# Two-layer GNN on one core: message rows and their places in a ring of eight slots, every scatter plain

## The reference, cut to what matters

```
weight = relu(edge_attr @ W1 + b1) @ W2 + b2      # edge_attr: (206250, 64), weight: (206250, 128)
h      = x @ Wl + bl                              # (6250, 128)
msg    = h[dst] * weight
out    = segment_sum(msg, src, 6250);  x = x + out
```

## Time and profile before

| | us |
|---|---|
| median of 3 runs | 3927.46 (3926.26 to 3931.88) |
| span of the profiled execution | 3952.0 |
| POOL busy | 2311.6 (58%), 1789 instructions |
| PE busy | 3250.2 (82%) |
| DVE busy | 2751.6 (70%) |
| ACT busy | 2038.0 (52%) |
| scatters, line 581 | 1664, the first at 1133.1, the last at 3801.1 |

### The profile page before, as it was taken

One profiled execution on the slowest core, in us unless ns is written; L12 is line 12 of the kernel. 1 busy time (PEld: TensorE's weight loads), 2 busy tenths in 40 slices (PEclk: granted clock), 3 DMA queues, 4 the chain that ended last, 5 costly groups with the idle time before them and its releaser, 6 DMA issues.

```text
span 3952.0 us, 95934 instructions
## 1 busy us (share of the span) xinstructions
PE 3250.2 (82%) x26010; PEld 2424.8 (61%) x26011; DVE 2751.6 (70%) x7605; ACT 2038.0 (52%) x4686; POOL 2311.6 (58%) x1789
## 2 busy tenths in 40 slices
PE   1899999999777778888888888888778787888867
PEld 0566666666555556665666666666566665666656
DVE  8888888888854456666666666666666666666746
ACT  3688788877532224444444444444444443444456
POOL 5200000000247778888888788888888888888830
PEclk9999999999867778998988888899899998899989
DMA  3398988200024457776667667677666676667757
GB/s 103 111 313 309 313 312 312 91 5 2 12 50 84 82 96 149 148 140 123 147 136 147 139 129 144 142 142 148 123 147 140 140 148 120 142 143 145 153 129 204
DMA packets 571932, 569.04 MB, mean 144 GB/s; under 512 B 69768, under 2 KB 555670, under 8 KB 571621
## 3 DMA queue, kind: packets, MB, share of 16 engines
q1 hardware_dynamic: 424950, 446.22, 40.5%
q0 software_dynamic: 146672, 119.07, 20.4%
HBM read 280.17 MB, written 284.85 MB: 143 GB/s over the span
## 4 chain that ended last, share of the span: by engine, by line
PE 50%; issue 16%; DVE 11%; ACT 5%; POOL 5%; another core or an unknown queue 5%; DMA 4%; DVEq 2%; ACTq 0%; POOLq 0%; SPq 0%
PE PS L1085 12%; PE PS L1246 10%; PE PS L1213 7%; PE PS L1225 5%; POOL messages L581 5%; PE PS L1076 4%; PE PS L1202 4%; DMA messages<-big,idxr 4%; ACT big L1425 2%; DVE aux L737 2%; DVE X L986 2%; PE PS L1210 2%; PE PS L1194 2%; ACT H L1429 1%
## 5 line engine op out<-in xcount | busy, mean ns | idle before, releaser
L581 POOL DMA_INDIRECT messages<-big,idxr x1664 | 2145.7, 1290 | 566.8 <-issue 480.1
L1246 PE MATMUL PS<-big,H 128*128 128x128 f32 x4800 | 657.4, 294 | 224.9 <-ACT H L1429 123.7
L1246 PEld LDWEIGHTS PS<-big,H 128*128 128x128 f32 x4800 | 614.0, 207 | 276.6 <-issue 237.9
L1413 ACT ACTIVATE big<-PS 128x512 f32<-128x512 f32 x416 | 248.4, 597 | 1002.4 <-PE PS L1225 615.8
L1085 PE MATMUL PS<-par,aux 128*128 128x386 bf16 x3626 | 682.4, 327 | 0.0
L959 DVE TENSOR_TENSOR big<-PS,big 128x512 f32<-128x512 f32 x416 | 287.3, 691 | 465.5 <-remote 213.0
L1330 ACT ACTIVATE aux<-PS 128x784 bf16<-128x784 f32 x592 | 480.4, 823 | 205.9 <-PE PS L1076 201.2
L1213 PE MATMUL PS<-W2s,big 128*128 128x128 f32 x3328 | 555.6, 317 | 0.0
L1213 PEld LDWEIGHTS PS<-W2s,big 128*128 128x128 f32 x3328 | 466.9, 217 | 109.3 <-issue 109.3
L986 DVE TENSOR_TENSOR X<-X,PS 128x128 f32 x1200 | 345.2, 288 | 247.6 <-PE PS L1246 88.8
L1402 ACT ACTIVATE big<-PS,b1c 128x512 f32<-128x512 f32 x416 | 283.3, 681 | 432.9 <-PE PS L1202 245.3
(11 more groups left out here) (221 smaller groups left out, 3769.9 us busy)
## 6 DMA issues: line engine op xcount, KB each, us to landing
messages<-zeros SPq DMA_DIRECT2D x843, 193.5 KB
big<-messages SPq DMA_DIRECT2D x300, 516.0 KB
aux<-slot_rows SPq DMA_DIRECT2D x416, 128.0 KB
big<-in_edge_attr_dram SPq DMA_DIRECT2D x402, 128.0 KB
messages<-big,idxr POOLq DMA_INDIRECT x1664
X<-in_x_dram SPq DMA_DIRECT2D x6, 448.0 KB, 11.4
out_dram<-X SPq DMA_DIRECT2D x6, 448.0 KB
edge_places<-big SPq DMA_DIRECT2D x1, 2496.0 KB, 13.2
```

The costliest lines, as they stand in the source:

```text
L581: pool.indirect_dma_start(strm_d, bass.IndirectOffsetOnAxis(ap=idxr[:, n % U, j:j + 1], axis=0), outr[:, n % U, j, :], None, compute_op=AL ...
L1246: last = nc.tensor.matmul(to[:, r * C:(r + 1) * C], finhot[:, n % 2, r * 2 + q, :], fin[:, k, r, q * ROW:q * ROW + C], start=(q == 0), sto ...
```

## The change

The rings of `outr` and `idxr` get UO = 8 slots, each with its semaphore, and `outr` moves from the tile `big` to a free piece of `H`. `ADDING` is empty, so all 1664 scatters write plainly. POOL's steps are 8 written out and one loop of 17 rounds of 24. On the other engines `steps` writes out 20 steps instead of 4 at the start of the first part, and its loop makes two rounds of 16 instead of three: the wait on a landed scatter then has a value above zero wherever it stands in a loop. The wait values follow from the eight semaphores. Everything else stays.

```diff
+    UO = 2 * U
+    ADDING = ()
-        idxr = sb("idxr", [P, U, J], i32)
+        idxr = sb("idxr", [P, UO, J], i32)
-        outr = part(big, used, U * J * ROW).rearrange("p (u j c) -> p u j c", u=U, j=J)
+        free_n = H[:, :, :].rearrange("p b c -> p (b c)")
+        outr = free_n[:, 2 * FO * P:2 * FO * P + UO * J * ROW].rearrange("p (u j c) -> p u j c", u=UO, j=J)
-        S_sc = [sem(f"scattered_{k}") for k in range(U)]
+        S_sc = [sem(f"scattered_{k}") for k in range(UO)]
...
         def steps(eng, step, turn=None, rings=RINGS):
-            for s in range(U):
+            for s in range(U + U * rings):
                 step(s, s, None)
             for p, rounds in enumerate(LOOPS):
-                at = U if p == 0 else TURN[p - 1] - 1
+                at = U + U * rings if p == 0 else TURN[p - 1] - 1
+                if p == 0:
+                    rounds = rounds - 1
...
             def part_landed(p):
-                for k in range(U):
-                    sp.wait_ge(S_sc[k], 64 * len(range(k, TURN[p], U)))
+                for k in range(UO):
+                    sp.wait_ge(S_sc[k], 64 * len(range(k, TURN[p], UO)))
...
                 for j in range(J):
-                    pool.indirect_dma_start(strm_d, bass.IndirectOffsetOnAxis(ap=idxr[:, n % U, j:j + 1], axis=0),
-                                            outr[:, n % U, j, :], None, compute_op=ALU.add if j in adding else ALU.bypass).then_inc(S_sc[n % U], 16)
+                    pool.indirect_dma_start(strm_d, bass.IndirectOffsetOnAxis(ap=idxr[:, n % UO, j:j + 1], axis=0),
+                                            outr[:, n % UO, j, :], None, compute_op=ALU.add if j in adding else ALU.bypass).then_inc(S_sc[n % UO], 16)
-            fewer = ((1,), (0, 3))
-            for g in range(U):
-                scatter(g, g, fewer[g % 2])
...
+            for g in range(UO):
+                scatter(g, g, ADDING)
...
+            with pool.Fori(0, (G - UO) // (3 * UO)):
+                for k in range(3 * UO):
+                    scatter(None, UO + k, ADDING)
...
             def row_places(g, n):
-                k, s = n % U, n % 2
+                k, s = n % UO, n % 2
...
-                wait(dve, S_sc[k], (g - k) * 16)
+                wait(dve, S_sc[k], (g - k) * (64 // UO))
                 nc.vector.tensor_copy(idxr[:, k, :], place_f).then_inc(S["rank_chain"], 1)
```

More of the change, by code:

```diff
@@ L32, in gnn_program @@
     GT = T0 // J
-    GL = (GT - 1 - U) // (3 * U)
     XS = T0 - (SB - 1) * P
-    assert GT * J == T0 and G % U == 0 and 0 < XS < P and XS + NB - 1 <= P
+    ADDING = ()
+    assert GT * J == T0 and G % U == 0 and (G - UO) % (3 * UO) == 0 and 0 < XS < P and XS + NB - 1 <= P
     TB = -(-T0 // P)
@@ L215, in gnn_program @@
         fin = part(big, used, 4 * FO * ROW).rearrange("p (s r f) -> p s r f", s=4, r=FO // 2)
-        finhot = H[:, :, :].rearrange("p b c -> p (b c)")[:, 0:2 * FO * P].rearrange("p (s t v) -> p s t v", s=2, t=FO)
+        free_n = H[:, :, :].rearrange("p b c -> p (b c)")
+        finhot = free_n[:, 0:2 * FO * P].rearrange("p (s t v) -> p s t v", s=2, t=FO)
+        outr = free_n[:, 2 * FO * P:2 * FO * P + UO * J * ROW].rearrange("p (u j c) -> p u j c", u=UO, j=J)
         par = sb("par", [P, NB * HW], bf16)
@@ L446, in _ @@
             steps(sp, edge_loads)
-            for k in range(U):
-                sp.wait_ge(S_sc[k], 16 * G)
+            for k in range(UO):
+                sp.wait_ge(S_sc[k], 64 * (G // UO))
             octs(sp, stream_loads)
@@ L566, in _, with scatter @@
             filled = pool.alloc_register("filled")
-            def scatter(g, n, adding=(1, 3)):
+            def scatter(g, n, adding):
                 if not isinstance(g, int):
@@ L580, in scatter @@
                 for j in range(J):
-                    pool.indirect_dma_start(strm_d, bass.IndirectOffsetOnAxis(ap=idxr[:, n % U, j:j + 1], axis=0),
-                                            outr[:, n % U, j, :], None, compute_op=ALU.add if j in adding else ALU.bypass).then_inc(S_sc[n % U], 16)
-            fewer = ((1,), (0, 3))
-            for g in range(U):
-                scatter(g, g, fewer[g % 2])
[L587 to L597, removed]
+                    pool.indirect_dma_start(strm_d, bass.IndirectOffsetOnAxis(ap=idxr[:, n % UO, j:j + 1], axis=0),
+                                            outr[:, n % UO, j, :], None, compute_op=ALU.add if j in adding else ALU.bypass).then_inc(S_sc[n % UO], 16)
+            for g in range(UO):
+                scatter(g, g, ADDING)
+            pool.reg_mov(placed, 5 * UO + 5)
+            pool.reg_mov(lrows, UO + 1)
+            pool.reg_mov(filled, UO + 1)
+            with pool.Fori(0, (G - UO) // (3 * UO)):
+                for k in range(3 * UO):
+                    scatter(None, UO + k, ADDING)
         def dve_link(eng, count):
@@ L958, in messages @@
                 dve.wait_ge(S["hgc_done"], g + 1)
-                nc.vector.tensor_tensor(outr[:, k, :, 0:C], pW[:, k % 2, :].rearrange("p (j c) -> p j c", j=J),
+                nc.vector.tensor_tensor(outr[:, n % UO, :, 0:C], pW[:, k % 2, :].rearrange("p (j c) -> p j c", j=J),
                                         hgs[:, k % 2, :].rearrange("p (j c) -> p j c", j=J), ALU.mult).then_inc(S["msg_done"], 1)
@@ L1406, in local_rows @@
                 act.wait_ge(S["rank_chain"], g * 5 + 5)
-                nc.scalar.activation(outr[:, k, :, C], blcol[:, 1, ds(g * J, J)], ACT.Copy, scale=-1.0).then_inc(S["lrow_ready"], 1)
+                nc.scalar.activation(outr[:, n % UO, :, C], blcol[:, 1, ds(g * J, J)], ACT.Copy, scale=-1.0).then_inc(S["lrow_ready"], 1)
             def rows_copy(g, n):
```

## The result

The changed kernel takes 4419.8 us (median of 4 runs, 4415.3 to 4423.9) where the kernel before takes 3928.2 us on the same chip: a ratio of 1.124 (95% interval 1.123 to 1.126), 12.4% slower. The forecast was 3832 us and the range ended at 3915 us, so the prediction was wrong in sign and size.

What follows compares the result with a forecast made beforehand. POOL's scatters looked like the bound, with the DVE, PE and ACT round next. Gains of 76 (ring wait), 15 (end) and 4 (turns) sum to 95 us: profiled 3952.0 becomes 3857, or 3832 us as median; range 3700 to 3915.

Steps and rivals of the forecast that it cites:

- What bounds the kernel: Layer 1: POOL's scatters look like the bound, 6.43 us a step, with the DVE, PE and ACT round nearly as slow.
- All scatters plain, POOL's cost: POOL in layer 1: 806 scatters fall from 1.56 to 0.97 us, saving 476 us of its time; 5.08 us a step.
- The round behind it: Later steps of layer 1: the DVE, PE and ACT round sets the pace next, near 6.22 us a step.
- Ring wait, half of 151.6 us: DVE's line 953 waiting for landed scatters: eight slots remove it, gaining 76 us (bounds 0 and 151.6).
- The end and the turns: After the last message, POOL's shorter lag saves 15 us; at turns between parts, SP's shorter wait saves 4 of 33.4 us.
- First part: First 52 steps: no gain, as messages already set 6.33 us a step; at most 65 us if wrong.
- DMA: Software queue and DMA engines in layer 1: plain scatters should need less of them; costed at nothing.
- Written-out steps, H, semaphores: Longer straight code, message rows in H, four more semaphores: 0, or 3 us better if a left-out return saves a stall.
- The free run: Rival, layer 1: without ring waits PE's clock rises, 5.5 us a step, 3572 us, half way about 3740; 13 in 100.
- The slower rival: Line 953's waits cover PE lateness that then shows at lines 959 and 986: 6.55 us a step, 3956 us; 8 in 100.

Runs made afterwards that it cites:

- half the rows: The changed kernel with the scatters for j = 2 and 3 left out: 3486.1 us, ratio 0.887 to the kernel before.
- the rests in the middle of a step: Changed kernel, POOL waiting for two memsets behind scatter j = 1 (387 columns, then 16, 128, 230 or 387): 4023.1, 4011.6, 4001.7, 4023.8 us.
- the one at its end: Changed kernel, POOL waiting for one memset of 387 columns behind the last scatter (j = 3) of each step: 4192.6 us, ratio 1.062.

## Why the prediction was wrong

*What bounds the kernel.* "It looks like the bound" was right: POOL is within 57 to 80 us of its floor, and removing the slot wait alone gives 1.000. But I then left this reading for the round of DVE, PE and ACT, on the strength of a sentence that is false, that this round "is nearly as slow as POOL". Free of long rows of scatters it makes a step in 5.53 us. The equal paces in the earlier trace rows were POOL's own pace, or nearly: 50 steps of 6.26 us are 313 of the 320 us.

*All scatters plain, POOL's cost.* Right: 0.97 us, 5.08 us a step.

*The round behind it: the step that failed.* "Everything else that a faster POOL may give must come through them or from the end" treated POOL's choice of scatter as a matter of POOL's time alone, and the round as untouched by it. The sum had no term for it; it put the round at 6.22 us a step. The runs showed a coupling that runs the other way: behind back-to-back plain scatters PE's signals come late (by 1.7 and 5.1 us in the table above), and a step takes 7.68 us. The trace of the kernel before had it in view. Its waits from 1300 to 3700 us hold these lines:

```profile
ACT big L1413 <- remote: 298.3, 98, 5.2
...
DVE big L959 <- remote: 163.0, 85, 5.9
```

One of them is ACT's 5.25 us at 2143.55 us, ended 0.04 us after an adding scatter. The prediction looked at named releasers only and uses none of these.

*Ring wait, half of 151.6 us.* Measured 0 (ratio 1.000, 0.999 to 1.001, with eight slots and adds). The lower bound that I had named was the truth; that the window without the wait was no faster said so.

*The end and the turns.* The end came as forecast: the last scatter ends 5.6 us behind the last message (4261.73 us). But it is worth nothing beside the rest. The first drain load starts 1.5 us after the last scatter's end,

```profile
4266.32 0.96 POOL L585 DMA_INDIRECT messages<-H,idxr  x1 [0.30 <-issue]
4268.73 2.33 SPq L414 DMA_DIRECT2D big<-messages  x4
```

and of the 15 us nothing shows in the run with the ring alone, since there POOL stays behind. The turns fell from 33.4 to 9.4 us without effect on a time that others set.

*First part.* "I take 0, cover: the message round" was wrong by 0.45 us in 52 steps, 23 us slower. POOL's wait for messages there rose from 18.6 to 72.8 us.

*DMA.* "I cost it at nothing" was right for the transfers: packets fell by 62% and the share of the DMA engines from 0.68 to 0.42.

*Written-out steps, H, semaphores.* Nothing, as said; the run with the ring of eight contains all of them. The Trainium skill (Runtime: NRT & Kernel Launch, Instruction fetch mechanics) has a taken branch out of the fetched pages wait for a fetch. No run here shows what the one return that is left out saves: the 3.4 us that a return cost in the earlier trace rows lie within that run's interval of 0.1%.

*The rivals.* The free run put the unhindered round at 5.5 us a step, and half the rows gave 5.53 us; but what hindered it was not the ring's wait. It also tied the clock to PE's waiting: the granted clock is 0.90 in the kernel before, 0.82 in the changed one, where the round waits for late signals, and 0.97 with half the rows. The slower rival had the right sign and the right line (957 waiting for its inputs), but it looked for hidden lateness of PE and priced it at 44 us; the lateness was made by the change itself and cost 492.

*What is shown and what is not.* Shown: the plain scatters alone cause it (ring of four, too); idle time of POOL removes most of it without adds; half the scatters, which means shorter rows and an idle POOL at once, remove it; PE's signals appear in bursts behind such rows, and those of DVE and ACT do not. Argued only: that the products had really run when the profile says so and just their signals were late. The ends of PE's products in the profile are modelled, so they do not prove it. For it speaks that PE's later products are recorded meanwhile and that the signals of several products appear 0.04 to 0.1 us apart (five of them between 2523.30 and 2523.55 us), among them that of the weights, whose product alone takes 1.16 us. Open is by what path POOL's scatters hold up PE and neither DVE nor ACT. It is not the scatter's packets at the DMA engines as far as the times go: behind the rows of four the first signal keeps its 1.0 us after POOL's end while the last packet ends 0.9 to 4 us after it. And why the rests in the middle of a step do more than the one at its end is open.

## What to carry to other kernels

When one engine is the bound because it issues many indirect transfers, making each cheaper also makes its rows denser; look first at whether other engines' waits with an unknown releaser end where its rows, or its slower instructions, end. If they do, the slow instructions may be openings, and the change should be tried at several doses and not all or none. And a wait of an engine that does not set the pace can be worth nothing: 151.6 us of waiting went here and the time stayed the same.

## What the runs showed of the hardware

- A plain indirect scatter of 128 message rows costs POOL 0.97 us and shows 16 packets of 4128 bytes in the trace; an adding one costs 1.56 us and shows 128 packets of 516 bytes.
- Between plain scatters at 1.27 us PE's signals are late by 1.7 us in the median 2 to 4.8 us into a row and by 5.1 us further on; POOL idle: 0.02 us. Those of DVE and ACT come within 0.02 us in either case.
- PE's signals come through about at the end of an adding scatter; with two apart in four the time is 57 to 80 us over POOL's floor, and one (ratio 1.116) is nearly as bad as none (1.124).
- A memset that POOL waits for costs it a gap of 1.14 us with one column and 1.46 us with 387, behind a scatter that ends a step; behind the second scatter 387 columns give 1.23 us and a second such memset 0.55 us more.
